# A loop written out, and the norm work of two head groups joined in one tile of six columns

## The reference, cut to what matters

```
dw = gradient of this chunk + Mom * mean(momentum)      # three 64x64 matrices a head
Mom = dw
X = dw / (sqrt(sum(dw*dw)) + 1e-7)                       # one norm for each matrix
for a, b, c in NS_COEFFS:                                # five steps
    A = X @ X.T;  B = b*A + c*(A@A);  X = a*X + B@X
W = W + X
W = W / (norm(W, axis=2) + 1e-5) * n                     # n: norms of the rows of the first W
```

## Time and profile before

| | us |
|---|---|
| median of three runs | 843.06 |
| the profiled execution, own time | 843.61 |
| its span | 841.8 |
| PE busy (matmul) | 785.6, 93% |
| DVE busy | 721.4, 86% |
| POOL busy | 407.2, 48% |
| ACT busy | 354.6, 42% |

### The profile page before, as it was taken

One profiled execution on the slowest core, in us unless ns is written; L12 is line 12 of the kernel. 1 busy time (PEld: TensorE's weight loads), 2 busy tenths in 40 slices (PEclk: granted clock), 3 DMA queues, 4 the chain that ended last, 5 costly groups with the idle time before them and its releaser, 6 DMA issues.

```text
span 841.8 us, 27295 instructions
## 1 busy us (share of the span) xinstructions
PE 785.6 (93%) x9776; PEld 671.7 (80%) x9776; DVE 721.4 (86%) x2592; ACT 354.6 (42%) x868; POOL 407.2 (48%) x535
## 2 busy tenths in 40 slices
PE   3899999999999999999999999999999999999997
PEld 2888888878887788878888788888888878888886
DVE  4789898897988979889798897988989888898865
ACT  2544344443444434444444444344343453433533
POOL 1654545445454454544554446544464544645442
PEclk9899999999999999999999999999999999999999
DMA  8100000000000000000000000000000000000000
GB/s 322 47 2 15 8 2 20 0 12 6 0 19 0 12 6 0 19 0 12 6 0 19 0 12 6 0 19 0 12 6 0 19 0 12 6 0 12 0 12 7
DMA packets 9716, 13.77 MB, mean 16 GB/s; under 512 B 1120, under 2 KB 8928, under 8 KB 9440
## 3 DMA queue, kind: packets, MB, share of 16 engines
q1 hardware_dynamic: 7904, 7.80, 3.2%
q10 hardware_dynamic: 1792, 5.70, 1.7%
HBM read 11.41 MB, written 2.10 MB: 16 GB/s over the span
## 4 chain that ended last, share of the span: by engine, by line
PE 51%; DVE 34%; issue 9%; ACT 2%; POOL 2%; DMA 1%; DVEq 1%; SPq 0%; ACTq 0%
PE CC L631 17%; PE M L631 12%; PE HB L631 10%; PE YB L631 8%; DVE acc L1330 7%; DVE Wn L1177 4%; DVE X L1148 2%; DVE dhb L1096 2%; DVE lt L1050 2%; POOL r L287 2%; DVE Am L1133 1%; PE CC L701 1%; DVE Mp L1140 1%; DMA rows<-in_rows 1%; PE CC L702 1%
## 5 line engine op out<-in xcount | busy, mean ns | idle before, releaser
L365 POOL TENSOR_TENSOR hq<-hr 128x512 f32<-128x512 f32 x128 | 136.9, 1069 | 77.6 <-ACT hr L428 76.1
L287 POOL TENSOR_TENSOR r<-r,half 128x3 f32<-128x3 f32 (+1 forms) x78 | 77.9, 1012 | 151.1 <-DVE r L1118 68.6
L631 PE MATMUL HB<-xlT,e_s 128*128 128x128 f32 x1024 | 144.2, 284 | 0.4 <-ACT xlT L428 0.4
L631 PE MATMUL YB<-e_s,hq 128*128 128x128 f32 x1024 | 142.1, 282 | 1.9 <-DVE acc L1330 0.8
L343 POOL TENSOR_TENSOR aX<-X,a_tile 128x192 f32<-128x192 f32 x150 | 93.1, 641 | 85.2 <-DVE X L1148 85.2
L631 PEld LDWEIGHTS HB<-xlT,e_s 128*128 128x128 f32 x1024 | 127.2, 194 | 7.7 <-ACT xlT L428 0.7
L1330 DVE SCALAR_TENSOR_TENSOR acc<-YB,cw,acc 128x128 f32<-128x128 f32 x448 | 125.5, 342 | 9.0 <-PE YB L631 9.0
L631 PEld LDWEIGHTS YB<-e_s,hq 128*128 128x128 f32 x1024 | 125.0, 192 | 7.4 <-issue 4.1
L428 ACT ACTIVATE hr<-HB 128x512 f32<-128x512 f32 x128 | 76.1, 595 | 129.7 <-PE HB L631 129.7
L631 PEld LDWEIGHTS CC<-Am 64*64 64x64 f32 x1800 | 60.8, 134 | 24.3 <-issue 19.8
L631 PEld LDWEIGHTS CC<-X,Mp 64*64 64x64 f32 x1800 | 58.8, 134 | 25.5 <-issue 23.7
(11 more groups left out here) (180 smaller groups left out, 1530.7 us busy)
## 6 DMA issues: line engine op xcount, KB each, us to landing
xa<-in_x SPq DMA_DIRECT2D x16, 128.0 KB, 2.0
e_s<-in_e1T ACTq DMA_DIRECT2D x1, 2048.0 KB, 12.9
e_s<-in_e2T ACTq DMA_DIRECT2D x1, 2048.0 KB, 19.2
xr<-in_x SPq DMA_DIRECT2D x16, 128.0 KB, 2.1
out<-ot SPq DMA_DIRECT2D x16, 128.0 KB, 1.7
wall<-in_wall SPq DMA_DIRECT2D x1, 820.0 KB, 5.8
up_s<-in_upT ACTq DMA_DIRECT2D x1, 512.0 KB, 14.3
down_s<-in_downT ACTq DMA_DIRECT2D x1, 512.0 KB, 19.7
```

Source lines behind the costliest of these rows:

```text
L287: return pool.tensor_tensor(dst, src, expo[:, 0:n], ALU.pow)
L365: pool.tensor_tensor(hq[b][:, :, :], hr[b][:, :, :], hr[b][:, :, :], ALU.mult).then_inc(e_hq, 1)
L631: return pe.matmul(out_, lhsT, rhs, start=start, stop=stop)
```

## The change

Two things are done. First, the loop over chunks 1 to 14 is written out on all five engines. The chunk's number is known when the program is made, every wait is for a constant, and `Expect` counts in the program that writes the kernel instead of in a register. Second, the small tiles of both groups are joined: `r3[0]` and `r3[1]` are now columns 0 to 2 and 3 to 5 of one tile `r6`, `nrm` has six columns, and sums, copy, power, addition and inverse are done once for six columns, behind waits for both groups. The scaling of Wn is no longer three `tensor_scalar` with two scalars a group: the inverses are multiplied by `nrm` (six columns), and then each group has one multiplication of 192 columns by the three factors, broadcast.

The core of the diff:

```diff
     def wait(self, skip=0):
-        self.eng.wait_ge(self.sem, self.reg)
-        self.eng.reg_add(self.reg, self.reg, self.step + skip)
+        self.eng.wait_ge(self.sem, self.due)
+        self.due += self.step + skip
...
-        r3 = [sb(f"r3{g}", [P, 6, 3]) for g in range(G)]
+        r6 = sb("r6", [P, 6, 3 * G])
+        r3 = [r6[:, :, 3 * g:3 * g + 3] for g in range(G)]
...
-            def ss_pow(i, g):
-                pool.wait_ge(e_sst[g], 3 * i + 1)
-                power(r3[g][:, 2, :], r3[g][:, 1, :], half, 3).then_inc(e_pw[g], 1)
+            def ss_pow(i):
+                pool.wait_ge(e_sst, 3 * i + 1)
+                power(r6[:, 2, :], r6[:, 1, :], half, 3 * G).then_inc(e_pw, 1)
...
-            def row_pow(m, g):
-
-                pool.wait_ge(e_rn[g], m + 1)
-                power(r3[g][:, 4, :], r3[g][:, 3, :], half, 3).then_inc(e_rp[g], 1)
+            def row_pow(m):
+                for g in range(G):
+                    pool.wait_ge(e_rn[g], m + 1)
+                power(r6[:, 4, :], r6[:, 3, :], half, 3 * G).then_inc(e_rp, 1)
...
-            def sums(i, g):
-                pe.wait_ge(e_s3[g], 2 * i + 2)
-                mm(CB[g][:, 0:3], bdones[:, :], r3[g][:, 0, :]).then_inc(e_ssb[g], 1)
+            def sums(i):
+                for g in range(G):
+                    pe.wait_ge(e_s3[g], 2 * i + 2)
+                mm(CB[0][:, 0:3 * G], bdones[:, :], r6[:, 0, :]).then_inc(e_ssb, 1)
...
-                for g in range(G):
-                    dve.wait_ge(e_pw[g], i + 1)
-                    nc.vector.tensor_scalar(r3[g][:, 2, :], r3[g][:, 2, :], 1e-7, None, ALU.add).then_inc(e_sst[g], 1)
-                    dve.wait_ge(e_sst[g], 3 * i + 2)
-                    nc.vector.reciprocal(r3[g][:, 1, :], r3[g][:, 2, :]).then_inc(e_sst[g], 1)
-                    dve.wait_ge(e_sst[g], 3 * i + 3)
+                dve.wait_ge(e_pw, i + 1)
+                nc.vector.tensor_scalar(r6[:, 2, :], r6[:, 2, :], 1e-7, None, ALU.add).then_inc(e_sst, 1)
+                dve.wait_ge(e_sst, 3 * i + 2)
+                nc.vector.reciprocal(r6[:, 1, :], r6[:, 2, :]).then_inc(e_sst, 1)
+                dve.wait_ge(e_sst, 3 * i + 3)
+                for g in range(G):
                     nc.vector.tensor_tensor(X[g][:, :, :], Mom[g][:, :, :],
...
-                    for w in range(3):
-                        ins = nc.vector.tensor_scalar(Wn[g][:, w, :], Wn[g][:, w, :], r3[g][:, 5, w:w + 1],
-                                                      nrm[g][:, w:w + 1], ALU.mult, ALU.mult)
-                    ins.then_inc(e_wn[g], 1)
+                nc.vector.tensor_tensor(r6[:, 5, :], r6[:, 5, :], nrm[:, :], ALU.mult).then_inc(e_rs, 1)
+                dve.wait_ge(e_rs, 3 * m)
+                for g in range(G):
+                    nc.vector.tensor_tensor(Wn[g][:, :, :], Wn[g][:, :, :],
+                                            r3[g][:, 5, :].unsqueeze(2).to_broadcast([P, 3, HD]), ALU.mult)\
+                        .then_inc(e_wn[g], 1)
...
-            with dve.Fori(1, LAST) as i:
+            for i in range(1, LAST):
                 body(i, False)
```

More of the change, by code:

```diff
@@ L65, in __init__ @@
     def __init__(self, eng, sem, name, first=1, step=1):
-        self.eng, self.sem, self.step = eng, sem, step
-        self.reg = eng.alloc_register(name)
-        eng.reg_mov(self.reg, first)
+        self.eng, self.sem, self.step, self.due = eng, sem, step, first
     def wait(self, skip=0):
-        self.eng.wait_ge(self.sem, self.reg)
-        self.eng.reg_add(self.reg, self.reg, self.step + skip)
+        self.eng.wait_ge(self.sem, self.due)
+        self.due += self.step + skip
 def build(nc, x, wall_d, rows_d, wo, fast_d, affine_d, fc1T, fc2T, e1T, e2T, upT, downT, ident_d, fixed_d, out):
@@ L115, in build @@
         Mom = [sb(f"Mom{g}", [P, 3, HD]) for g in range(G)]
-        nrm = [sb(f"nrm{g}", [P, 3]) for g in range(G)]
+        nrm = sb("nrm", [P, 3 * G])
         X = [sb(f"X{g}", [P, 3, HD]) for g in range(G)]
@@ L222, in build @@
         e_k, e_kc, e_kd, e_ku, e_dgr = (per_group(n) for n in ("k_side", "k_copied", "k_steps", "k_u", "dgba"))
-        e_dw, e_G, e_s3, e_ssb, e_sst, e_pw, e_x = (per_group(n) for n in ("dw", "G", "s3", "ssb", "sst", "pw", "X"))
+        e_dw, e_G, e_s3, e_x = (per_group(n) for n in ("dw", "G", "s3", "X"))
+        e_ssb, e_sst, e_pw, e_rp, e_rs = (sem(n) for n in ("ssb", "sst", "pw", "rp", "row_scale"))
         e_ax, e_t, e_xt, e_am = (per_group(n) for n in ("aX", "turn", "XT", "Am"))
         e_prod, e_mp = (per_group(n) for n in ("product", "Mp"))
-        e_up, e_rn, e_rp, e_wn, e_bd, e_wt, e_WT = (per_group(n) for n in ("upd", "rn", "rp", "Wn", "W1BD", "wt", "WT"))
+        e_up, e_rn, e_wn, e_bd, e_wt, e_WT = (per_group(n) for n in ("upd", "rn", "Wn", "W1BD", "wt", "WT"))
         e_qs, e_gsig, e_gt1, e_gh, e_qo, e_to = (sem(n) for n in ("q_side", "gate_sig", "gt1", "gh", "q_out", "to_copied"))
@@ L261, in store @@
                 sp.dma_start(out[bass.ds(rows, P), :], ot[:, :]).then_inc(e_stored, 16)
-            with sp.Fori(0, NT - 2) as i:
-                here, after, later = sp.snap(i * P), sp.snap((i + 1) * P), sp.snap((i + 2) * P)
+            for i in range(NT - 2):
+                here, after, later = i * P, (i + 1) * P, (i + 2) * P
                 sp.wait_ge(e_xn, i + 2)
@@ L377, in body @@
                 m = i + 1
-                first = isinstance(i, int)
+                first = i == 0
                 k_u(i, 0)
@@ L381, in body @@
                 h_sq(i, 1)
[L382 to L383 removed]
+                ss_pow(i)
                 prep_rstd(m)
@@ L397, in body @@
                         f()
-                for g in range(G):
-                    row_pow(m, g)
+                row_pow(m)
                 h_sq(m, 0)
             prep_rstd(0)
-            for g in range(G):
-                row_pow(0, g)
+            row_pow(0)
             prep_n8(0)
@@ L410, in _ @@
             body(0, False)
-            with pool.Fori(1, LAST) as i:
+            for i in range(1, LAST):
                 body(i, False)
@@ L612, in _ @@
             body(0, False)
-            with act.Fori(1, LAST) as i:
+            for i in range(1, LAST):
                 body(i, False)
@@ L908, in body @@
                 shared_up(i, 0)
-                sums(i, 0)
-                sums(i, 1)
+                sums(i)
                 shared_up(i, 1)
@@ L963, in _ @@
             body(0, False)
-            with pe.Fori(1, LAST) as i:
+            for i in range(1, LAST):
                 body(i, False)
@@ L1367, in body @@
                 grad(i)
-                sum_copy(i, 0)
-                sum_copy(i, 1)
+                sum_copy(i)
                 x_first(i)
@@ L1400, in _ @@
             row_sums(0)
-            for g in range(G):
-                dve.wait_ge(e_rp[g], 1)
-                nc.vector.tensor_copy(nrm[g][:, :], r3[g][:, 4, :]).then_inc(e_up[g], 2)
+            dve.wait_ge(e_rp, 1)
+            nc.vector.tensor_copy(nrm[:, :], r6[:, 4, :])
             w_bd(0)
```

20 lines of the change are left out of this document (10 added, 10 removed).

## The result

The changed kernel takes 845.86 us (median of 7 runs, 845.3 to 846.9), the kernel before 843.06 (7 runs beside them, 840.7 to 843.85). The ratio is 1.004, with an interval from 1.0026 to 1.0055: slower by 0.4%, where 838.5 was forecast. The profiled execution took 845.8 us for a span of 843.9.

The account below looks back on a forecast made before the run. The bound was taken to be one chunk's chain of waits, where PE and DVE take turns. Terms of -4.8 - 3.0 + 5.1 - 1.5 - 0.9 = -5.1 against 843.6 gave 838.5 us, range 831 to 852.5.

Parts of the forecast that it names:

- (d): Second norm joined: addition and inverse fit in ahead of `hq`; 0.1 a chunk, 1.5 us less in all.
- (a): Loop over chunks: its arithmetic goes, 0.34 a chunk in 14 chunks, 4.8 us less.
- (b): Waits in all chunks: the register counters of `Expect` go, 0.2 a chunk, 3.0 us less.
- (c): First norm joined: longer power makes X0 0.476 later, against two hops of 0.07; net 0.34 a chunk, 5.1 us more.
- (e): Second norm of chunk 14, once: the second group's products are no longer held up, 0.9 us less.
- rival 2: Second norm: `hq` starts ahead of the addition and holds it, 0.35 a chunk, 843.7 us, no change; chance 0.16.
- (f): Branches: back edges cost nothing visible, and the prologue's joined power lies beside the loading of constants; no term.
- rival 4: Written-out code must be fetched, one 2.0 us fetch a chunk, 30 us more, 868 us; chance 0.03.
- Rival 3: Loop registers are hidden and chunk 0's 0.34 is pipeline start, so (a) and (b) give nothing: 846.3 us; chance 0.08.
- The weighing of the broadcast product: Second norm's scaling: 0.36 for 192 columns by the rows, against the skill's rule of 1.52 a group, some 22 us more.

Follow-up runs that it names:

- run 1: The kernel before with its loop written out and counters as constants, nothing joined: 831.17 us, ratio 0.9853.
- run 3: The kernel before, written out, with only the first norm joined: 839.85 us, ratio 0.996.
- run 4: The kernel before, written out, with only the second norm joined, with the broadcast product: 836.8 us, ratio 0.9919.
- run 5: The changed kernel with GpSimd's `hq` behind the second norm waiting until both groups' weights are scaled: 834.73 us, ratio 0.9899.
- run 8: The kernel before, written out, norms apart, second norm's scaling as one broadcast multiplication a group: 825.28 us, ratio 0.9788.
- run 7: run 1 with `hq` behind the second norm waiting until both groups' weights are scaled: 826.69 us, ratio 0.9811.
- run 10: run 8 with hq(m,0) waiting for the copies into W1BD and hq(i,1) for the second group's dga: 809.12 us, ratio 0.9597.
- run 6: The changed kernel with GpSimd's one-column rstd power ahead of the first norm's six-column power: 858.12 us, ratio 1.0178.
- run 2: The changed kernel with the hardware loop and register counters put back, both norms joined: 848.76 us, ratio 1.0063.

## Why the prediction was wrong

Its direction was wrong through one step, (d), the second norm. The measured sizes are differences of medians, of runs 1 to 4 on one chip; the sum is that of the result:

| step | forecast | measured |
|---|---|---|
| written out: (a), (b) and the two hops that (c) had set against itself | -4.8 - 3.0 - 2.1 = -9.9 | -12.5 (run 1), of which 1.4 by the clock |
| (c) first norm joined, without those hops | +0.476 x 15 = +7.1 | +8.7 (run 3 less run 1) |
| (d) second norm joined | -1.5 | +5.6 (run 4 less run 1) |
| (e) second norm of chunk 14 | -0.9 | inside the rows above |
| left over | | +1.0 |
| sum | -5.2 | +2.8 |

- **(a)** was right: 0.34 forecast from chunk 0 against chunk 2, 0.32 found.
- **(b)** came near. With the two hops that stand in (c) the counters were given 0.2 + 0.14 = 0.34 a chunk, and 0.41 was found in chunk 0. The 0.2 itself was a guess between bounds of 0 and 0.5, so that this is in part luck.
- **(c)** had the right mechanism. The power was right within 0.02 us. That PE's one matmul of the sums now waits for both groups was in no term: 0.12. X0 came 0.61 later, where 0.476 was forecast.
- **(d)** is the step that failed. It had "the addition and the inverse fit in ahead of `hq`". In the changed kernel `hq` is ahead of the addition in all 15 chunks. Counted from the reductions' end, Wn0 was to be ready 2.97 us behind it and came at 498.56 - 495.20 = 3.36; Wn1 was to come at 3.24 and came at 3.63. Both are 0.39 late, by rival 2's mechanism and close to its 0.35. Run 5 shows that it is the cause: without the hold-up the kernel takes 834.7. A second, small error is the weighing of the two groups. Measured from the end of the reductions, joining makes Wn0 0.75 later (3.36 for 2.61), Wn1 0.06 earlier (3.63 for 3.69) and the next gate product 0.43 later (9.88 for 9.45, run 4 and run 1). That fits group 0, which PE and ACT take first, counting for six tenths (0.75 x 0.6 - 0.06 x 0.4 = 0.43), an estimate that run 5 bears out (0.07 and 0.89 earlier, gate 0.40). The forecast's -0.1 between +0.29 and -0.52 had made it half, which is 0.07 a chunk; the hold-up is 0.39.
- The prediction gave rival 2 a chance of 0.16 on a margin of 0.01 us: 442.34 for `hq` and 442.33 for the addition, which by these numbers is ahead, though the text calls it behind. The margin had been worked out from `hq`'s start in a looped chunk, although the change takes the register from GpSimd's wait for `hr` too. The trace of before had the other start in it, in chunk 0, which is written out:

```profile
75.60 1.67 POOL L287 TENSOR_TENSOR r<-r,half 128x3 f32<-128x3 f32 x2 [3.02 <-DVE r L1158]
...
77.23 1.10 POOL L365 TENSOR_TENSOR hq<-hr 128x512 f32<-128x512 f32 x1
```

Here `hq` starts 0.04 ahead of the power's modelled end (77.27); in the 14 looped chunks it starts 0.10 behind it (442.48 for 442.38). With the start of chunk 0 `hq` would have stood at 442.27, ahead of the addition at 442.33, and rival 2 would have been the forecast. At the first norm GpSimd's next instruction starts ahead of such an end even in the loop: 455.38 for 455.41, and `hq` 455.90 for 455.94. In all traces `hq`, when `hr` is there and its wait is on a constant, starts 0.03 to 0.04 ahead of the end of the power before it, and DVE's dependent addition never came first.
- **(e)** had the right mechanism. In chunk 14 Wn1 is ready 3.63 behind the reductions instead of 4.49, and the next gate product is 0.52 earlier against them (7.32 for 7.84), 0.31 by the writing out and 0.21 by the joining, where 0.9 was forecast.
- **(f)** and rival 4: code loading went from 12 packets on q8 to 78 and shows no gap of 2 us a chunk; run 1 is the fastest of the first four with the same 78. Two chunks of the changed kernel are some 0.3 longer than the others (52.68 and 52.73 for 52.40), and so are two of run 3; fetching may be the reason, and no run tested that. Rival 3 is out by run 1.
- The weighing of the broadcast product was right. The Trainium skill, "VectorE: DVE Perf Modes", perf-mode tier table, would have it at half the rate; at 192 columns one product takes 0.36 (run 8) and three scalings 0.76 (run 7), and run 8 gains. The rule doesn't decide at this size.

## What to carry to other kernels

Where an engine's small instruction depends on GpSimd's result, look at what GpSimd does next: if it is a long elementwise operation from SBUF that is ready, it started first wherever its wait was on a constant, and held the small one on DVE for its whole length. Let it wait for the end of the chain, or put a harmless instruction between. Push such work to a place where DVE reads PSUM (run 10), not to the next step of the same chain (run 7). Joining two short operations into one saves only if neither result was needed early: here the first group's lead was worth more than the instruction saved, while one broadcast multiplication for three small ones was worth having.

## What the runs showed of the hardware

- A GpSimd multiplication of 128x512 float32 (1.04 us) holds a DVE operation on SBUF that starts behind it until it ends, however small that one is: an addition on 6 columns takes 1.00 instead of 0.17 (runs 4 and 6), a copy of 64 columns 0.92 instead of 0.18 (run 7), a product of 128 columns 1.12 instead of 0.28 (runs 8 and 10). A GpSimd power doesn't: beside it additions keep their 0.17 and the product of 192 columns its 0.36. DVE operations with an input in PSUM aren't held (run 10). The Trainium skill, "GPSIMD Engine Reference", section Specifications, names who contends, and the multiplications here agree with it; the powers are an exception to it that these runs show.
- The same edit costs 5 us in a loop (run 2) and some 15 written out (+2.8 for the whole change, less the -12.5 of run 1). By the chunk it is 0.54 (52.68 for 52.14) and 1.03 (52.40 for 51.37). Of the 0.49 between them 0.39 lies at the second norm, where `hq`'s start moves by 0.1 us against the end of the power and the race is decided by 0.05.
- GpSimd's next instruction starts 0.03 to 0.04 us ahead of the modelled end of the power before it, if its data are there. At the second norm of looped chunks `hq` starts 0.10 (before) and 0.08 (run 2) behind that end, and in chunk 0 of the same traces 0.04 ahead. At the first norm it isn't late in the loop either (455.90 for 455.94), so that the loop costs GpSimd something at one place and not at the other; why is not shown.
- The power on GpSimd costs by the column: 555 ns for one (the changed kernel), 851 for three, 1345 for six, 1637 for eight.
